# Gated decay attention of a decoder megakernel: scores from three products of rounded parts, rotary sums in one place, exponents of the second sequence moved

## What is computed

```python
q, k, v = hidden @ Wq.T, hidden @ Wk.T, hidden @ Wv.T      # by heads
q, k = rope(q), rope(k)                                    # x * cos + rotate_half(x) * sin
dt = softplus(hidden @ Win.T + dt_bias); G = cumsum(dt * -exp(A_log_bias))    # per chunk
scores = einsum('bhnid,bhnjd->bhnij', qc, kc)
decay = where(causal, exp(G[i] - G[j]), 0)
y_intra = einsum('bhnij,bhnjd->bhnid', scores * decay, xc)   # xc = v * dt
# y_inter: the state of the chunk before, decayed
y = (y_intra + y_inter) / rms * gnorm_w
y = y * silu(hidden @ Wg.T)
return y @ Wo.T
```

## Time and profile before

| what | value |
| --- | --- |
| median of 3 runs | 1468.35 us (1467.91 to 1472.45) |
| profiled execution | 1467.15 us |
| its span in the profile | 1465.0 us |
| mean granted TensorE clock | 0.991 |
| PE / DVE / ACT / POOL busy | 96% / 74% / 58% / 41% |
| the gated decay attention | about 530 to 960 us of the span, 53.0 us per middle group |

### The profile page before, as it was taken

How to read it: one execution, slowest core, us unless ns; L and a number is a source line. 1 busy time by engine, 2 the same in 40 slices (tenths; PEclk the granted TensorE clock), 3 DMA queues, 4 the chain that set the end, 5 groups by cost and what they waited for, 6 DMA issues and landing times.

```text
span 1465.0 us, 24269 instructions
## 1 busy us (share of the span) xinstructions
PE 1407.8 (96%) x7610; PEld 1167.8 (80%) x7610; DVE 1090.4 (74%) x2485; ACT 854.6 (58%) x2146; POOL 604.5 (41%) x633
## 2 busy tenths in 40 slices
PE   7999999999989989999999999879999999999997
PEld 6788888887778867787778778668888888888873
DVE  5697667697688877767776776767788788788884
ACT  4556555655223157656755755648677677677660
POOL 4555444444022137556655745435243243242110
PEclk9999999999999999999999999999999999999999
DMA  8011110102122341330321321310111022012000
GB/s 323 1 73 72 73 63 9 72 33 102 58 87 87 114 135 55 103 128 30 130 100 47 111 101 58 129 73 30 40 63 73 15 73 86 15 72 78 1 0 29
DMA packets 30133, 107.72 MB, mean 74 GB/s; under 512 B 3847, under 2 KB 13191, under 8 KB 22104
## 3 DMA queue, kind: packets, MB, share of 16 engines
q1 hardware_dynamic: 30040, 106.58, 20.1%
HBM read 97.07 MB, written 9.50 MB: 73 GB/s over the span
## 4 chain that ended last, share of the span: by engine, by line
PE 53%; DVE 17%; issue 16%; POOL 8%; ACT 4%; DMA 1%; POOLq 0%; DVEq 0%; SPq 0%; ACTq 0%
PE bank L186 11%; PE bank L187 10%; PE bank L188 10%; PE bank L1774 3%; POOL yss L1407 2%; PE bank L316 2%; PE bank L1789 2%; PE bank L339 2%; PE bank L1795 2%; PE bank L1791 2%; POOL tmp L159 1%; PE bank L1231 1%; PE bank L1732 1%; PE bank L327 1%; PE bank L285 1%
## 5 line engine op out<-in xcount | busy, mean ns | idle before, releaser
L159 POOL TENSOR_TENSOR tmp<-tmp,sin 128x512 f32<-128x512 f32 x80 | 111.5, 1394 | 211.2 <-ACT tmp L152 211.2
L188 PE MATMUL bank<-wo_low,att_high 128*128 128x512 f32 x384 | 150.7, 392 | 0.0
L2073 DVE SCALAR_TENSOR_TENSOR logit<-bank,qss,amask 128x512 f32<-128x512 f32 x128 | 90.9, 747 | 57.0 <-PE bank L188 55.9
L1986 POOL TENSOR_TENSOR qss<-qss,half 128x4 f32<-128x4 f32 x32 | 34.9, 1090 | 199.6 <-DVE qss L2059 199.6
L1607 PE MATMUL bank<-kT,wg 128*128 128x256 f32 x512 | 113.1, 383 | 4.0 <-ACT prob L1641 4.0
L1893 ACT ACTIVATE prob<-logit,rmax 128x512 f32<-128x512 f32 x128 | 91.6, 719 | 37.8 <-DVE rmax L2077 37.8
L1607 PEld LDWEIGHTS bank<-kT,wg 128*128 128x128 f32 x512 | 98.1, 192 | 17.9 <-ACT prob L1641 4.4
L186 PE MATMUL bank<-l_wo_high,att_high 128*128 128x512 f32 x256 | 104.7, 409 | 1.8 <-DVE att_low L1491 1.1
L187 PE MATMUL bank<-xT_high,wq_low 128*128 128x512 f32 x256 | 102.3, 400 | 0.0
L187 PE MATMUL bank<-l_wo_high,att_low 128*128 128x512 f32 x256 | 99.8, 390 | 0.0
L1907 ACT ACTIVATE p_high<-bank 128x512 fp32r<-128x512 f32 x128 | 70.1, 597 | 46.4 <-PE bank L1774 46.1
(11 more groups left out here) (270 smaller groups left out, 4414.1 us busy)
## 6 DMA issues: line engine op xcount, KB each, us to landing
wq<-in_l_wq SPq DMA_DIRECT2D x16, 1024.0 KB, 6.6
wo<-in_l_wo SPq DMA_DIRECT2D x16, 1024.0 KB, 5.0
wkv<-in_l_wkv SPq DMA_DIRECT2D x16, 512.0 KB, 5.7
wg<-in_l_wg SPq DMA_DIRECT2D x8, 1024.0 KB, 4.8
wq<-in_x_wq SPq DMA_DIRECT2D x8, 1024.0 KB, 7.2
wo<-in_x_wo SPq DMA_DIRECT2D x8, 1024.0 KB, 4.9
kT<-in_x_wkv SPq DMA_DIRECT2D x8, 512.0 KB, 4.2
kv_keys<-logit SPq DMA_DIRECT2D x8, 512.0 KB, 4.6
```

The lines of the kernel that those rows point to most:

```text
L159: eng.tensor_tensor(halves(tmp[4 + j % 2]), halves(tmp[2 + j % 2]), per_batch(sin), ALU.mult).then_inc(sem(f"{l}_sinp"), 1)
L188: return eng.matmul(dst, a_high, b_low, start=False, stop=stop)
L2073: dve.scalar_tensor_tensor(logit[s % 2][:, c, :], bank[3 + c][:, :], qss[p][:, 1, h, 2 * b + c:2 * b + c + 1], amask[:, c, :], ALU.mult, A ...
```

## The change

- The scores are made by `product` from high and low parts of q and k: nine fp32r matmuls for each sequence in place of three FP32 ones.
- Rotated q and k of every group are written to `kT[1]` and `qT[1]`; the high parts lie in `kT0` and `qT0`, the low parts overwrite the rotated values in place. `l1_rope_sum` waits, for j = 0 and 1, until all scores of the group before are done.
- ACT makes the high part of each rotated tile (`l1_round`, 128x512 copy), DVE the low part (`l1_rounded_rest`, 128x512 subtraction), five of each per group. scores(0) waits for the fifth low part.
- On DVE exponents(1,0) and exponents(1,1) move behind all four sums, between and behind the last subtractions. On ACT the roundings stand after copies 3 and 4, around decays(0), and, for the next key, between headed(1) and squares(3). Ahead of group 0, ACT's rounding of the key stands before the copy to `cols`.
- Four semaphores of the Sinkhorn start become two, and `dt_turn` is merged into `dt`.

```diff
-                dve.tensor_tensor(t4, src, wide(mx), ALU.subtract).then_inc(sem("sink_in"), 1)
-                dve.wait_ge(sem("sink_exp"), side + 1)
+                dve.tensor_tensor(t4, src, wide(mx), ALU.subtract).then_inc(sem("sink_vector"), 1)
+                dve.wait_ge(sem("sink_scalar"), 2 * side + 1)
...
+        l1_q = [over("l1_q_high", [P, GH, T], "qT0"), over("l1_q_low", [P, GH, T], "qT1")]
+        l1_k = [over("l1_k_high", [P, T], "kT0"), over("l1_k_low", [P, T], "kT1")]
+
+        def l1_part(i, j):
+            return l1_k[i][:, :] if j == 0 else l1_q[i][:, j - 1, :]
+
+        def l1_rotated(j):
+            return kT[1][:, 0:T] if j == 0 else qT[1][:, j - 1, :]
+
+        def l1_rope_sum(dve, g, j):
+            if j < 2 and due(6 * g):
+                dve.wait_ge(sem("l1_score"), 6 * g)
+            rope_sum(dve, "l1", g, j, l1_rotated(j))
+
+        def l1_round(act, g, j):
+            act.wait_ge(sem("l1_rope"), 5 * g + j + 1)
+            act.activation(l1_part(0, j), l1_rotated(j), ACT.Copy).then_inc(sem("l1_high"), 1)
+
+        def l1_rounded_rest(dve, g, j):
+            dve.wait_ge(sem("l1_high"), 5 * g + j + 1)
+            dve.tensor_tensor(l1_part(1, j), l1_rotated(j), l1_part(0, j).bitcast(F32), ALU.subtract)\
+               .then_inc(sem("l1_low"), 1)
...
-                                pe.wait_ge(sem("l1_rope"), 5 * g + 5)
+                                pe.wait_ge(sem("l1_low"), 5 * g + 5)
...
-                        pe.matmul(bank[3 + m][:, :], kT[p][:, b * L + kt * P:b * L + (kt + 1) * P],
-                                  qT[p][:, :, b * L + qt * P:b * L + (qt + 1) * P], start=True, stop=True)\
-                          .then_inc(sem("l1_score"), 1)
+                        product(pe, bank[3 + m][:, :],
+                                [k[:, b * L + kt * P:b * L + (kt + 1) * P] for k in l1_k],
+                                [q[:, :, b * L + qt * P:b * L + (qt + 1) * P] for q in l1_q], True, True)\
+                            .then_inc(sem("l1_score"), 1)
...
-                for j in range(GH):
-                    rope_psum_copies(act, "l1", g, j + 1, bank[(j + 1) % 2])
+                for j in range(1, GH + 1):
+                    rope_psum_copies(act, "l1", g, j, bank[j % 2])
+                    if j > 2:
+                        l1_round(act, g, j - 2)
+                l1_round(act, g, GH - 1)
                 decays(0)
+                l1_round(act, g, GH)
                 decays(1)
...
                 headed(1)
+                if not last_group:
+                    l1_round(act, n, 0)
                 squares(3)
...
             value(0, 0, bank[4])
-            act.wait_ge(sem("dt_turn"), 1)
+            l1_round(act, 0, 0)
+            act.wait_ge(sem("dt"), 2)
...
-                if due(6 * (g - 1)):
-                    dve.wait_ge(sem("l1_score"), 6 * (g - 1))
-                rope_sum(dve, "l1", g, 1, qT[p][:, 0, :])
+                l1_rope_sum(dve, g, 1)
+                l1_rope_sum(dve, g, 2)
+                l1_rounded_rest(dve, g, 1)
+                l1_rope_sum(dve, g, 3)
+                l1_rounded_rest(dve, g, 2)
+                l1_rope_sum(dve, g, 4)
+                l1_rounded_rest(dve, g, 3)
                 exponents(1, 0)
-                rope_sum(dve, "l1", g, 2, qT[p][:, 1, :])
+                l1_rounded_rest(dve, g, 4)
                 exponents(1, 1)
-                rope_sum(dve, "l1", g, 3, qT[p][:, 2, :])
-                rope_sum(dve, "l1", g, 4, qT[p][:, 3, :])
...
-                    if due(6 * g):
-                        dve.wait_ge(sem("l1_score"), 6 * g)
-                    rope_sum(dve, "l1", n, 0, kT[1 - p][:, 0:T])
+                    l1_rope_sum(dve, n, 0)
                 gated(2)
+                if not last_group:
+                    l1_rounded_rest(dve, n, 0)
                 mean(3)
...
-            rope_sum(dve, "l1", 0, 0, kT[0][:, 0:T])
+            l1_rope_sum(dve, 0, 0)
+            l1_rounded_rest(dve, 0, 0)
```

More of the change, by code:

```diff
@@ L845, in mix_vector @@
                 step(dve, dve.tensor_reduce(vec4(mx), lines, AX.X, ALU.max))
-                dve.tensor_tensor(t4, src, wide(mx), ALU.subtract).then_inc(sem("sink_in"), 1)
-                dve.wait_ge(sem("sink_exp"), side + 1)
+                dve.tensor_tensor(t4, src, wide(mx), ALU.subtract).then_inc(sem("sink_vector"), 1)
+                dve.wait_ge(sem("sink_scalar"), 2 * side + 1)
                 t_lines = t4 if side == 0 else rows4(ztmp[:, :, :], True)
-                dve.tensor_reduce(vec4(zsm[:, 2, :]), t_lines, AX.X, ALU.add).then_inc(sem("sink_sum"), 1)
-                dve.wait_ge(sem("sink_ln"), side + 1)
+                dve.tensor_reduce(vec4(zsm[:, 2, :]), t_lines, AX.X, ALU.add).then_inc(sem("sink_vector"), 1)
+                dve.wait_ge(sem("sink_scalar"), 2 * side + 2)
                 step(dve, dve.tensor_tensor(ls, ls, mx, ALU.add))
@@ L975, in sink_scalar @@
             for side in range(2):
-                act.wait_ge(sem("sink_in"), side + 1)
-                act.activation(z, z, ACT.Exp).then_inc(sem("sink_exp"), 1)
-                act.wait_ge(sem("sink_sum"), side + 1)
-                act.activation(zsm[:, 1, :], zsm[:, 2, :], ACT.Ln).then_inc(sem("sink_ln"), 1)
+                act.wait_ge(sem("sink_vector"), 2 * side + 1)
+                act.activation(z, z, ACT.Exp).then_inc(sem("sink_scalar"), 1)
+                act.wait_ge(sem("sink_vector"), 2 * side + 2)
+                act.activation(zsm[:, 1, :], zsm[:, 2, :], ACT.Ln).then_inc(sem("sink_scalar"), 1)
             act.wait_ge(sem("mix_ready"), 1)
@@ L1083, in dt_turn @@
                 last = pe.transpose(bank[5][:, n * 32:(n + 1) * 32], src[:, at:at + P], ident[0:32, 0:32])
-            last.then_inc(sem("dt_turn"), 1)
+            last.then_inc(sem("dt"), 1)
         def dt_scalar(act):
```

## The result

| | before | after |
| --- | --- | --- |
| median | 1469.3 us (5 runs) | 1512.97 us (5 runs, 1510.49 to 1515.06) |
| ratio after / before | | 1.0284, 95% interval 1.0268 to 1.0300 |
| profiled execution, span | 1467.15 us, 1465.0 us | 1510.49 us, 1508.3 us |
| mean granted TensorE clock | 0.991 | 0.981 |

The change makes the kernel slower by 2.8%. The sign was forecast, the size was not: 1498 us was predicted, 1480 to 1507 the range.

The account below looks back on a forecast made before the run. It took TensorE and the equally critical chain through sigmoid(0), wq_low and z(1) to bound the kernel. Six middle groups at 4.1 us (3.3 + 0.8), first 5.0, last 1.1 gave +30.7: 1498 us, range 1480 to 1507.

Parts of the forecast that it names:

- What bounds the kernel: Whole kernel: TensorE busy 96% of the span, with the chain clamp(0), sigmoid(0), wq_low, z(1) as critical.
- The gain: Score products on TensorE: nine rounded for three FP32 save some 0.55 us per block, 16 blocks, 8.8 us in all.
- Sum 4 does not move: DVE's rotary sums: subtractions 1 and 2 fill the room left by the moved exponents; sum 4 still ends at 766.26.
- plus what POOL's eight 128-wide pieces cost ... up to 0.5: DVE between sum 4 and scores(0): contention adds 0.1 to 0.2 us each, up to 0.5, to 2.36 us.
- The third rival: Six DVE instructions behind sum 4 each wait 0.40 us for a POOL piece: 1.6 us more per group, 1509; chance 0.08.
- the walk: Step-by-step timing of one middle group: scores(0) 2.5 us later, outputs 3.3 us later.
- Sigmoid(0) and z(1): Chain on ACT, POOL and DVE: sigmoid(0) 4.3 us later; z(1) ends at 789.1, the output product starts 3.3 later.
- DVE's `wo_low`, which shared the port with it, is over by 779: DVE and POOL before power(0): wo_low no longer overlaps wq_low, which then needs 5.05 us, not 5.84.
- The clock: TensorE behind its wait before scores(0): a wait of 2.4 to 2.8 us was forecast, with no clock term.
- The tail: End of a group: the key's rounding on ACT before squares(3) delays the transposes of z(3), +0.8 us per group.
- First and last group: First group: late copy 1 behind the key's rounding, +5.0 us in all; last group, without wq_low: +1.1 us.
- The sum: Whole kernel: six middle groups at 4.1 us, 24.6, first 5.0, last 1.1, together +30.7 us, giving 1498.

Follow-up runs that it names:

- the products alone: Kernel before with its three FP32 score matmuls replaced by nine rounded products of other tiles, same waits, no roundings or subtractions: 1466.26 us, ratio 0.9971.
- the clock kept up: Changed kernel with 14 more rounded products per group before the wait for the last low part, keeping TensorE busy: 1506.08 us, ratio 1.0249.
- POOL's split out of the way: Changed kernel with POOL's split of the next key weights moved late, behind gated(0): 1505.35 us, ratio 1.0244.
- the exponents back: Changed kernel with exponents(1,0) and exponents(1,1) on DVE back behind sums 1 and 2, roundings and subtractions kept: 1510.55 us, ratio 1.0284.

## Why the prediction was wrong in size

- **What bounds the kernel.** Right. The chain through sigmoid(0), wq_low and z(1) is as critical as TensorE: the products alone turned half of their gain into a wait of 0.6 us before outputs(1,1).
- **The gain.** Right in the main at full clock (blocks of 2.16 to 2.21 us against 2.58 to 2.67: 0.4 to 0.5 each, not 0.55). It was worth 4 us alone, and 0.5 us per ordinary middle group inside the changed kernel.
- **Sum 4 does not move.** Right to 0.03 us, and with it the reading that the exponents only made room.
- **"plus what POOL's eight 128-wide pieces cost ... up to 0.5".** This term failed. Subtraction 3, the exponents and subtraction 4 took 3.5 us, not 2.4 to 2.9; scores(0) came 3.55 late, not 2.5. The two rows I priced it by were of 128x512 instructions, which lose 0.1 to 0.2 each; four exponents in sequence lose 0.8, the two subtractions 0.2 each. With POOL's split out of the way the same six take 2.3 us. The third rival (2.4 us lost by the six) was too high, the truth, 1.2, lay between. The rival also says that I had charged 0.8, where the walk charges up to 0.5; from 0.5 its price is 1.9 us per group and its time 1511, near the measured one, but not for its reason.
- **Sigmoid(0) and z(1).** Sigmoid(0) came 5.0 late, not 4.3: the same term, passed on. With the clock kept up power(0) is 3.9 late, not 3.3.
- **"DVE's `wo_low`, which shared the port with it, is over by 779".** This step failed as well: it was to be over 29.6 us into the group and ended at 31.4, and wq_low took 5.47 us instead of 5.05. With the clock kept up wo_low is over at 29.3 and wq_low takes 5.07, so the cause is the next point.
- **The clock.** Missing from the prediction altogether: a term put at nothing. A forecast wait of 2.5 us was written down without asking what TensorE's clock does behind it. It costs 1.3 us on the block, so that TensorE alone is 4.0 us late at the outputs instead of 1.4; 0.6 per group reach the period, through wo_low, and 2 more in the stray group.
- **The tail.** +0.8, measured 0.8 (5.29 less 4.51); removing it gave 0.7 per group.
- **First and last group.** First +8.6, predicted +5.0, last +2.5, predicted +1.1. Copy 1 was forecast 2.7 late, and I then took 0.9 for the group on the ground that sums would cover the rest; TensorE idled 5.7 us there (2.2 before), and went on at the low clock. Part of the 8.6 may not be the change: the kernel with nine products of other tiles starts its first group at 530.4, 1.3 us before the kernel before, and it lasts 59.4 us there, 0.7 more.
- **The sum.** The groups took 14.9 us more than forecast: 9.9 in the middle six (six times 0.7 for the contention behind sum 4, six times 0.6 for the clock, 2 for the stray group), 3.6 in the first, 1.4 in the last. The 2.2 us ahead of the first group come off: 43.3 us between the spans against 30.7 forecast.

## What to carry to other kernels

A gain on the busiest engine is worth what the next chain leaves of it: look for an instruction that starts with no wait just as its input arrives, and price the chain behind that too. When work is added to DVE in a stretch where POOL is active, count the instructions with two SBUF inputs, not their time. When a forecast puts a wait of some microseconds on TensorE, price the work behind it at the lower clock as well, and then look which long instructions of two other engines are pushed onto each other by it.

## What I had not expected of the hardware

- TensorE's fall to 1.2 GHz (products 0.43 us apart instead of 0.23) behind the wait for the low parts: after 3.67 to 3.76 us without work in all seven groups of the changed kernel that have such a wait, at once or up to four products later, and for six to thirteen products; after 3.16 to 3.33 us in all six such groups with the exponents back, after 2.64 us there not, after 2.55 us again; after 2.11 to 2.20 us in five of eight groups with the split late; after 0.44 to 0.47 us in none of seven groups with TensorE kept busy.
- Two runs of subtractions, one on DVE and one on POOL, that take 2.5 and 5.0 us alone take 5.25 and 6.16 together.
- Mean(0), an instruction of 128x4 that takes 0.16 us, took 1.10 after the change and ended with POOL's wq_low. Mean(2) did so too, 1.28 us, to 815.52, beside a sine product of POOL that ended at 815.50. So this form, with one input in SBUF, waited for POOL as well.
